# Edge passes of a graph network: PE waits for the chunk that a step needs, counted by SP, and reads its words from memory in every step

## The reference

```
msg = h[src] * norm[:, None]
out = jax.ops.segment_sum(msg, dst, num_segments=n)
```

## Time and profile before

| | |
|---|---|
| three runs | 6101.72, 6118.77, 6122.69 us |
| the profiled execution | 6087.99 us, span 6086.2 us |
| PE busy | 4655.6 us (76%), 13320 matmuls |
| POOL busy | 4038.2 us (66%) |
| DVE, ACT busy | 3512.5 us (58%), 2590.8 us (43%) |
| PE's matmuls of L1130 | 4980 (two a step), 2582.2 us busy |
| POOL's gathers of L1103 | 2346, 946 and 945 ns mean |
| mean granted clock of PE | 0.696 of full speed |

### The profile page before, as it was taken

One profiled execution on the slowest core, in us unless ns is written; L12 is line 12 of the kernel. 1 busy time (PEld: TensorE's weight loads), 2 busy tenths in 40 slices (PEclk: granted clock), 3 DMA queues, 4 the chain that ended last, 5 costly groups with the idle time before them and its releaser, 6 DMA issues.

```text
span 6086.2 us, 70752 instructions
## 1 busy us (share of the span) xinstructions
PE 4655.6 (76%) x13320; PEld 2535.9 (42%) x13320; DVE 3512.5 (58%) x10769; ACT 2590.8 (43%) x7522; POOL 4038.2 (66%) x4116
## 2 busy tenths in 40 slices
PE   5899988837888888988888863887888856666663
PEld 3667666623333334633333331333333623333331
DVE  4767787783333335833333347555555767777777
ACT  1655566554444444444444453000000456666664
POOL 2776677727777773067777755777777177777772
PEclk8877798775655667966565665656565977777776
DMA  4433343334333331033333322333333122222221
GB/s 128 107 106 96 96 107 107 101 96 119 105 105 106 106 105 50 33 105 106 106 105 105 106 62 82 105 106 105 105 105 105 36 54 53 53 53 53 53 53 55
DMA packets 237655, 539.07 MB, mean 89 GB/s; under 512 B 68266, under 2 KB 120424, under 8 KB 237242
## 3 DMA queue, kind: packets, MB, share of 16 engines
q0 software_dynamic: 180176, 481.36, 29.2%
q1 hardware_dynamic: 57066, 53.19, 2.7%
HBM read 498.15 MB, written 36.14 MB: 88 GB/s over the span
## 4 chain that ended last, share of the span: by engine, by line
PE 64%; issue 14%; DVE 12%; ACT 5%; POOL 2%; DMA 1%; DVEq 1%; ACTq 0%; POOLq 0%
PE bank L1130 40%; PE bank L1526 10%; PE bank L957 8%; PE bank L814 4%; PE bank L802 2%; DVE reg_acc L1152 1%; DVE scratch L183 1%; DVE scratch L201 1%; POOL scratch L1103 1%; DVE reg_acc L985 1%; ACT scratch L1541 1%; DVE scratch L1242 1%; ACT scratch L1546 1%; DVE scratch L1245 1%; DVE scratch L1233 1%
## 5 line engine op out<-in xcount | busy, mean ns | idle before, releaser
L1130 PE MATMUL bank<-scratch 128*128 x4980 | 2582.2, 634 | 668.3 <-issue 279.3
L1152 DVE TENSOR_TENSOR reg_acc<-reg_acc,bank 128x256 f32 x2490 | 1049.6, 422 | 1803.2 <-PE bank L1130 1779.7
L1130 PEld LDWEIGHTS bank<-scratch 128*128 128x128 f32 x4980 | 1147.9, 281 | 2102.5 <-issue 2077.3
L1103 POOL DMA_INDIRECT scratch<-tab_x,src_idx x1564 | 1479.5, 946 | 513.9 <-issue 383.8
L1111 ACT ACTIVATE scratch<-iota_row,dst_loc 128x128 f32<-128x128 f32 x1660 | 660.7, 401 | 1084.7 <-PE bank L1130 1066.0
L1103 POOL DMA_INDIRECT scratch<-tab_h,src_idx x782 | 739.3, 945 | 494.6 <-DMA tab_h<-reg_acc 256.7
L1499 POOL DMA_INDIRECT scratch<-tab_h,src_idx x832 | 856.1, 1029 | 263.8 <-issue 162.1
L710 POOL DMA_INDIRECT reg_x<-tab_h,src_idx x832 | 809.4, 973 | 301.0 <-issue 174.3
L1526 PE MATMUL bank<-scratch 128*128 128x260 f32 x1664 | 676.8, 525 | 425.9 <-issue 403.9
L957 PE MATMUL bank<-reg_x,scratch 128*128 128x265 f32 x1664 | 639.8, 495 | 102.3 <-DVE reg_x L994 60.5
L1526 PEld LDWEIGHTS bank<-scratch 128*128 128x128 f32 x1664 | 326.7, 242 | 743.4 <-issue 702.3
(11 more groups left out here) (229 smaller groups left out, 4430.7 us busy)
## 6 DMA issues: line engine op xcount, KB each, us to landing
scratch<-tab_h,src_idx POOLq DMA_INDIRECT x1614, 2.7
scratch<-tab_x,src_idx POOLq DMA_INDIRECT x1564, 2.7
reg_x<-tab_h,src_idx POOLq DMA_INDIRECT x832
reg_x<-in_x SPq DMA_DIRECT2D x12, 896.0 KB, 11.0
tab_h<-scratch SPq DMA_DIRECT2D x7, 924.0 KB, 4.5
tab_x<-reg_acc SPq DMA_DIRECT2D x7, 896.0 KB
tab_h<-reg_acc SPq DMA_DIRECT2D x7, 896.0 KB
tab_x<-reg_x SPq DMA_DIRECT2D x7, 896.0 KB
```

The costliest lines, as they stand in the source:

```text
L1103: e.indirect_dma_start(ring_rows[:, j % SLOTS, :], None, self.table, bass.IndirectOffsetOnAxis(ap=src_idx[:, j:j + 1], axis=0)).then_inc(* ...
L1130: e.matmul(psum[i % EDGE_BANKS][:, 0:FEAT], ring_hots[:, i % HOTS, :], slot_rows(e, i), start=True, stop=True).then_inc(*self.product.up)
L1152: e.tensor_tensor(v, v, psum[i % EDGE_BANKS][:, 0:FEAT], ALU.add).then_inc(*self.added.up)
```

## The change

The word that PE reads for a step now holds two numbers: the offset of the slot as before, and above it, times 65536, the number of chunks that must have landed, which is the step's chunk plus one (`landed_of`, made once at the start by one more instruction of DVE). In every step PE's sequencer reads eight words that begin at its own step, uses the first, takes the offset out of it (`slot_rows`) and the number of chunks (`chunks_needed`), and waits until the semaphore `pass_landed` has reached that number, a value in a register. Nobody but SP raises that semaphore: `EdgePass.sync` waits for chunk after chunk, now on 64 semaphores in turn, and adds one for each. POOL's wait and its gathers are as before. DVE asks for the address of its tile ahead of its waits. The numbers below the diff's `@@` are of the two files.

```diff
+ARRIVALS = 64
+PLACES = 2 ** 16
+WORDS = 8
...
-        s_slot = [signal(f"slot{k}_gathered", 16) for k in range(AHEAD)]
+        s_slot = [signal(f"arrival{k}", 16) for k in range(ARRIVALS)]
+        s_landed = [signal(f"pass{k}_landed") for k in (1, 2, 3)]
...
-            e.tensor_scalar(slot_i, slot_of, float(FEAT), None, ALU.mult).then_inc(*pre_v.done("slot_i"))
+            e.tensor_scalar(landed_of, chunk_of, 1.0, float(PLACES), ALU.add,
+                            ALU.mult).then_inc(*pre_v.done("landed_of"))
+            e.wait_ge(*pre_v.at("landed_of"))
+            e.scalar_tensor_tensor(out=slot_i, in0=slot_of, scalar=float(FEAT), in1=landed_of, op0=ALU.mult,
+                                   op1=ALU.add).then_inc(*pre_v.done("slot_i"))
...
-            n = min(GROUP, STEPS - t0)
+            n = min(WORDS, STEPS_PAD - t0)
             e.load(slot_regs[0:n], slot_row[:, t0:t0 + n])
 
-        def slot_rows(e, t):
-            v = e.snap(slot_regs[t % GROUP], min_val=0, max_val=(SLOTS - 1) * FEAT)
+        def slot_rows(e):
+            e.reg_alu(part_regs[0], slot_regs[0], PLACES - 1, op=ALU.bitwise_and)
+            v = e.snap(part_regs[0], min_val=0, max_val=(SLOTS - 1) * FEAT)
             return scratch[:, bass.DynSlice(v, FEAT)]
+
+        def chunks_needed(e):
+            e.reg_alu(part_regs[1], slot_regs[0], 16, op=ALU.logical_shift_right)
+            return e.snap(part_regs[1], min_val=1, max_val=CHUNKS)
...
+            def sync(self, e):
+                for j in range(CHUNKS):
+                    e.wait_ge(*self.got[j % ARRIVALS](j // ARRIVALS))
+                    e.sem_inc(*self.landed_n.up)
...
                 for i in range(STEPS):
-                    if i % GROUP == 0:
-                        load_slots(e, i)
+                    load_slots(e, i)
+                    rows, needed = slot_rows(e), chunks_needed(e)
                     if self.weighted:
                         e.wait_ge(*self.hot(i))
                     else:
                         e.wait_ge(*self.hot4(i // 4))
-                    if i < CHUNKS:
-                        e.wait_ge(*self.got[i % AHEAD](i // AHEAD))
                     if i >= EDGE_BANKS:
                         e.wait_ge(*self.added(i - EDGE_BANKS))
-                    e.matmul(psum[i % EDGE_BANKS][:, 0:FEAT], ring_hots[:, i % HOTS, :], slot_rows(e, i),
+                    e.wait_ge(self.landed.sem, needed)
+                    e.matmul(psum[i % EDGE_BANKS][:, 0:FEAT], ring_hots[:, i % HOTS, :], rows,
                              start=True, stop=True).then_inc(*self.product.up)
...
+                    v = sums_of(e, i, 0, FEAT)
                     e.wait_ge(*self.product(i))
                     if i:
                         e.wait_ge(*self.added(i - 1))
-                    v = sums_of(e, i, 0, FEAT)
...
             pass1_sync(e)
+            edges1.sync(e)
             close1_sync(e)
             pass2_sync(e)
+            edges2.sync(e)
             close2_sync(e)
+            edges3.sync(e)
             close3_sync(e)
```

More of the change, by code:

```diff
@@ L316, in build @@
         slot_i = small[:, 370:370 + STEP_BLOCKS].bitcast(I32)
+        landed_of = small[:, 380:380 + STEP_BLOCKS]
         chunk_i = reg_a[0:1, 0:CHUNKS].bitcast(I32)
@@ L351, in build @@
             "iota_row part ident step_no ones_row x_tail end_tile bound bounds hits0 hits1 hits2 hits3 hits4 hits5 hits6 "
-            "chunk_of chunk_idx tile_of first_node tile_i lap_16 lap slot_of slot_i prod_src w_src prod_dst w_dst tile_f tiles_half tiles_all "
+            "chunk_of chunk_idx tile_of first_node tile_i lap_16 lap slot_of landed_of slot_i prod_src w_src prod_dst w_dst tile_f tiles_half tiles_all "
             "n_steps n_less n_groups "
@@ L638, in load_tiles @@
             e.load(tile_regs[name][0:n], tile_row[0:1, t0:t0 + n])
-        slot_regs = []
+        slot_regs, part_regs = [], []
         def load_slots(e, t0):
             if not slot_regs:
-                slot_regs.extend(e.alloc_register(f"slot{k}") for k in range(GROUP))
-            n = min(GROUP, STEPS - t0)
+                slot_regs.extend(e.alloc_register(f"slot{k}") for k in range(WORDS))
+                part_regs.extend(e.alloc_register(f"part{k}") for k in range(2))
+            n = min(WORDS, STEPS_PAD - t0)
             e.load(slot_regs[0:n], slot_row[:, t0:t0 + n])
-        def slot_rows(e, t):
-            v = e.snap(slot_regs[t % GROUP], min_val=0, max_val=(SLOTS - 1) * FEAT)
+        def slot_rows(e):
+            e.reg_alu(part_regs[0], slot_regs[0], PLACES - 1, op=ALU.bitwise_and)
+            v = e.snap(part_regs[0], min_val=0, max_val=(SLOTS - 1) * FEAT)
             return scratch[:, bass.DynSlice(v, FEAT)]
+        def chunks_needed(e):
+            e.reg_alu(part_regs[1], slot_regs[0], 16, op=ALU.logical_shift_right)
+            return e.snap(part_regs[1], min_val=1, max_val=CHUNKS)
         def tile_value(e, name, t):
@@ L1085, in build, with __init__ @@
         class EdgePass:
-            def __init__(self, table, weighted):
+            def __init__(self, table, weighted, landed):
                 self.table, self.weighted = table, weighted
-                self.got = [s_slot[k].take(len(range(k, CHUNKS, AHEAD))) for k in range(AHEAD)]
+                self.landed = landed
+                self.landed_n = landed.take(CHUNKS)
+                self.got = [s_slot[k].take(len(range(k, CHUNKS, ARRIVALS))) for k in range(ARRIVALS)]
                 self.product, self.added = s_edge.take(STEPS), s_added.take(STEPS)
@@ L1104, in gpsimd @@
                         ring_rows[:, j % SLOTS, :], None, self.table,
-                        bass.IndirectOffsetOnAxis(ap=src_idx[:, j:j + 1], axis=0)).then_inc(*self.got[j % AHEAD].up)
+                        bass.IndirectOffsetOnAxis(ap=src_idx[:, j:j + 1], axis=0)).then_inc(*self.got[j % ARRIVALS].up)
+            def sync(self, e):
+                for j in range(CHUNKS):
+                    e.wait_ge(*self.got[j % ARRIVALS](j // ARRIVALS))
+                    e.sem_inc(*self.landed_n.up)
             def scalar(self, e):
@@ L1159, in build @@
         loads1 = s_load.take(5)
-        edges1 = EdgePass(tab_x1, False)
+        edges1 = EdgePass(tab_x1, False, s_landed[0])
         turn_ring = reg_a[:, 0:4 * P]
@@ L1262, in build @@
         loads2 = s_load.take(8)
-        edges2 = EdgePass(tab_h2, False)
+        edges2 = EdgePass(tab_h2, False, s_landed[1])
         w3_t = t_order.named("attn w00 w01 w10 w11")
@@ L1375, in close2_sync @@
                 e.dma_start(store_lot(tab_x2, a), lot(x_sb, a)).then_inc(*x2_stored.up)
-        edges3 = EdgePass(tab_x2, True)
+        edges3 = EdgePass(tab_x2, True, s_landed[2])
         dense_l2 = Dense((s_turned, s_kept, s_product), lambda j: sums[:, j, :], 2, wl2, FEAT, turn_ring, (0, 1, 2, 3),
```

## The result

The changed kernel takes 8430.88 us (median; 8412.0 to 8451.8), the kernel before in the same session 6120.73 us (one run at 6786 us is a disturbed one and left out of the ratio). The ratio is **1.379 (95% interval 1.374 to 1.384)**: 38% slower, where 6024 us, 1.6% faster, was forecast. The profiled execution takes 8428.55 us, its span is 8426.7 us.

A forecast was written before the change was run, and what follows sets the result against it. POOL's gathers at 1.250 us a chunk were taken as the bound, with PE's step of 0.285 + 0.60 + 0.19 = 1.08 us fitting under 1.178 us. Saving 95 us from 6118.8 gave 6024 us, range 5990 to 6050 us.

The forecast's parts named there:

- Bound and tail: Each pass: POOL's gathers at 1.250 us bound it; the 35.0 us tail shrinks to 3.1 us, saving 95 us in all.
- The wait against a register: PE's wait in each step: costs nothing beyond the old wait, with 0.095 us as upper end.
- rival 2: PE's wait against a register costs a share more, step 1.17 to 1.21 us, kernel 6072 us; chance 0.09.
- PE is the bound: Sign in the profile that the forecast is wrong: PE's wait L1153 nearly always at its shortest.
- Register arithmetic: PE's added REGISTER_ALU and one more ISA in each step: 0.19 us for both.
- The read of eight words: PE's read in each step: 0.60 us, taken from DVE's row for eight words.
- break-even of 1.214 us: PE's step time above which every pass is longer than before, whatever POOL does.
- The bound from above: PE's read of eight words: at most sixteen words' 1.11 us.
- nothing worth counting: PE's last five steps, reading 7 to 3 words: perhaps 0.2 us more each, 1.28 us against 1.25.
- Rival 1: PE's sequencer becomes the bound and the kernel slower: 6258 us, about 7750 us with every bound against it; chance 0.16.
- A step at the end of a tile is made up over 16 chunks: PE's additional step for the same chunk sets it back 1.08 us, regained at 0.17 us a chunk.

The follow-up runs named there:

- e14: Changed kernel with PE reading one word in each step instead of eight; 0.985 (0.980 to 0.989) of the kernel before.
- e6: Changed kernel with PE reading eight words, from a multiple of eight, only in every eighth step; 0.983 (0.980 to 0.986) of the kernel before.
- e7: Changed kernel with each step reading the eight words that begin at the multiple of eight below its own; 0.984 (0.980 to 0.988) of the kernel before.
- e13: Changed kernel's count without its wait: PE waits for constant count i + 1 in step i, sixteen words read every sixteenth step; 1.001 of the kernel before.
- e9: Kernel before with reads of 1 to 16 words from each step's own word, on PE in pass 1, DVE in pass 2; 1.104 of the kernel before.
- e4: Same kernel as e6, on a chip where the kernel before takes 7.0 ms; 1.007 of the kernel before.

## Why the prediction was wrong, point by point

1. **Bound and tail**: right. POOL's 1.250 us a gather was the bound, and the 35 us behind the last landing came from waiting for chunk i instead of chunk i - tile. e14 saves 98.9 us in the passes and e6 91 us, where the forecast had 95; 0.9845 of 6120.7 us is 6026 us, 0.984 (e7) 6021 us. e13 shows that it is this wait alone.
2. **The wait against a register**: nothing, as forecast. Its record of 51 ns and the 55 ns behind it are the same in e13, where the wait is for a constant, so rival 2 falls. The sign that I named for "PE is the bound", L1153 at its shortest, was no sign: it is at 51 ns in e14 too. The Trainium skill (Advanced Engine Details and Errata, Network/Comms) gives 50 to 100 ns for a sequencer's reading of a semaphore; no row here shows such a reading by itself, and 51 ns for a whole wait, with a register or a constant, leaves nothing to add for the register.
3. **Register arithmetic**: forecast 0.19 us, measured 0.257 us (rest of the step 0.541 for 0.285 us). From one start to the next in PE's sequencer, REGISTER_ALU takes 0.09 us, as assumed, and the added ISA, 0.112 us long itself, 0.17 us. Too low by 0.07 us, and harmless in itself: with an aligned read the step is 1.14 us, still under 1.178 us.
4. **"The read of eight words ... I take the row with the same count, 0.60 us": this step failed.** It measured 0.60 us in two steps of eight and 1.93 us in six, 1.60 us in the mean. With it the step is 1.60 + 0.54 = 2.14 us, far over the break-even of 1.214 us, and the pass runs at PE's pace. The bound from above failed with it: sixteen words' 1.11 us held only for reads that begin at a multiple of four words, which all those of the earlier trace rows do, because the kernel before reads at multiples of sixteen (L1687, of eight). That the changed kernel begins a read at every word was in the diff, and I compared counts alone. A row did show that the price is not one of counts: 1341 ns for fourteen words, more than the 1107 ns for sixteen. e9 resolves it: 853 ns for twelve and 495 ns for two words left over (835 - 340, six words less four) are 1.35 us. I had called this "nothing worth counting". The Trainium skill (Runtime: NRT & Kernel Launch, Instruction fetch mechanics) gives about 200 ns for each register, even in bulk, for the register loads that go in around a kernel at its launch; carried over to these reads, whose table lies in on-chip memory, an estimate by it is 1.6 us for eight words. I did not weigh it. The runs come near it for the starts off a multiple of four (0.233 us a word on PE) and not for the others (1107 ns for sixteen words, 0.07 us a word).
5. **Rival 1** (PE's sequencer is the bound) is what happened, with the break-even as worked out. I gave it 16%, and 7750 us at its worst; the real step, 2.14 us, lies above its 1.87 us.
6. **"A step at the end of a tile is made up over 16 chunks"**: true at 1.14 us (e7), void at 2.14 us. There PE is always behind: POOL's gather waits for the product of 12 steps before, so at the last gather 12 + 48 = 60 steps are open; 60 x 2.14 = 128 us, near the tail of 126.9 us.

## What to carry to other kernels

Take a read's price from rows with the same start as well as the same count: a read of words into registers from a multiple of four words costs a third of one from any other place once it has eight words. Where one word is needed in a step, read one, or read an aligned group once and let its registers last. And when two rows of a trace contradict the price that one uses (fourteen words dearer than sixteen), resolve that before summing.

## What the hardware showed that I had not expected

- The law of the first word in reads into registers, on PE and DVE: sixteen words take 1.107 us from a multiple of four words and 3.80 us from any other start (e9). Words up to the next multiple of four are not read singly with the rest in fours; the whole read goes word by word.
- On PE and on DVE alike a read goes on beside the product or sum ahead of it, and nothing of it is hidden from the engine's sequencer: the next step starts a read and 0.287 us later on PE, a read and 0.26 us later on DVE (medians of e9).
- A wait against a register costs PE's sequencer no more than one against a constant (51 ns each, e14 and e13), and these 51 ns can stand in the profile while the engine does wait: they are all that L1153 shows in e14.
- The same program runs at 6.1 ms on some chips and at 7.0 ms on others, at nearly the same granted clock in the passes (0.69 in e6, 0.68 in e4), and the order of two kernels can turn over between them (e6 0.983, e4 1.007).
